# Two triangular products of a grouped convolution in five sets of matmuls instead of six

## What is computed

```python
def conv_layer(x, c, weight, c_weight, bias):          # layers 0 and 2
    out = lax.conv_general_dilated(x, weight, window_strides=(1,), padding=[(4, 4)],
              dimension_numbers=('NCH', 'OIH', 'NCH'), feature_group_count=4)
    return out + jnp.einsum('nd,od->no', c, c_weight)[:, :, None] + bias[None, :, None]

def mix_layer(x, embedding, W0, b0, W1, b1, W2, b2, weight, bias_k):   # layers 1 and 3
    h = gelu(gelu(embedding @ W0 + b0) @ W1 + b1)
    att = jax.nn.softmax(h @ W2 + b2, axis=-1)
    agg_w = jnp.einsum('bk,koi->boi', att, weight[..., 0])
    return jnp.einsum('boi,bih->boh', agg_w, x) + (att @ bias_k)[:, :, None]

x = x + conv_layer(x, ...)
x = x + mix_layer(x, ...)
x = x + conv_layer(x, ...)
x = x + mix_layer(x, ...)
```

## Time and profile before

| | |
|---|---|
| median of 3 runs | 2541.18 us (2540.11 to 2541.45) |
| the profiled execution | 2542.88 us |
| its span, first to last instruction | 2541.0 us |
| mean granted TensorE clock over the span | 0.991 of 2.4 GHz |
| PE busy | 2491.0 us (98%), 45292 matmul instructions |
| DVE busy | 2134.1 us (84%) |
| ACT busy | 1519.8 us (60%) |
| DMA engines, mean busy share | 45% |

### The profile page before, as it was taken

How to read it: one execution, slowest core, us unless ns; L and a number is a source line. 1 busy time by engine, 2 the same in 40 slices (tenths; PEclk the granted TensorE clock), 3 DMA queues, 4 the chain that set the end, 5 groups by cost and what they waited for, 6 DMA issues and landing times.

```text
span 2541.0 us, 99176 instructions
## 1 busy us (share of the span) xinstructions
PE 2491.0 (98%) x45292; PEld 1381.1 (54%) x45292; DVE 2134.1 (84%) x811; ACT 1519.8 (60%) x1113; POOL 33.6 (1%) x31
## 2 busy tenths in 40 slices
PE   5999999999999999999999999999999999999998
PEld 3444444444444455555555566666666666666665
DVE  3679888888988988988988988988888898898883
ACT  3356666666666666666666666666666666666654
POOL 5000000000000000000000000000000000000000
PEclk9899999999999999999999999999999999999999
DMA  7534445444344344444443444444444544434433
GB/s 218 199 126 157 132 126 162 125 136 153 124 147 142 124 157 131 132 154 126 140 149 124 148 140 124 155 134 125 160 128 131 158 124 142 147 124 152 136 93 117
DMA packets 185506, 357.27 MB, mean 141 GB/s; under 512 B 12714, under 2 KB 143794, under 8 KB 152634
## 3 DMA queue, kind: packets, MB, share of 16 engines
q1 hardware_dynamic: 184576, 352.37, 44.3%
q10 hardware_dynamic: 898, 4.39, 0.8%
HBM read 205.72 MB, written 150.99 MB: 140 GB/s over the span
## 4 chain that ended last, share of the span: by engine, by line
PE 96%; DVE 1%; DMA 1%; ACT 1%; issue 1%; ACTq 0%; DVEq 0%
PE psum L338 60%; PE psum L404 35%; DMA mix_dram<-y 1%; PE psum L319 1%; DVE diff L644 0%; ACT y L541 0%; PE psum L311 0%; DVE y L707 0%; ACT y L569 0%; DVE att_t L669 0%; DVE y L698 0%; ACT x L608 0%; ACT outb L590 0%; ACT shared L551 0%; ACT shared L558 0%
## 5 line engine op out<-in xcount | busy, mean ns | idle before, releaser
L338 PE MATMUL psum<-diff,prod_w 32*64 32x512 f32 x28672 | 1691.2, 590 | 9.2 <-ACT shared L558 3.8
L338 PEld LDWEIGHTS psum<-diff,prod_w 32*64 32x64 f32 x28672 | 886.9, 132 | 719.5 <-issue 436.2
L644 DVE TENSOR_TENSOR diff<-xin 128x2052 f32<-128x2052 f32 x256 | 993.4, 3934 | 297.9 <-PE psum L338 297.4
L404 PE MATMUL psum<-y,mixw 32*64 32x512 f32 x16384 | 1022.9, 591 | 6.0 <-DVE y L707 5.3
L404 PEld LDWEIGHTS psum<-y,mixw 32*64 32x64 f32 x16384 | 533.8, 132 | 386.1 <-issue 232.1
L644 DVE TENSOR_TENSOR diff<-x 128x2055 f32<-128x2055 f32 x256 | 572.3, 2315 | 9.2 <-ACT x L608 9.2
L608 ACT ACTIVATE x<-psum,bias_now 128x2048 f32<-128x2048 f32 x128 | 253.2, 1978 | 207.8 <-PE psum L404 207.8
L590 ACT ACTIVATE outb<-psum,bias_now 128x2048 f32<-128x2048 f32 x128 | 252.1, 1969 | 200.4 <-PE psum L404 191.3
L558 ACT COPY shared<-psum 128x2048 f32<-128x2048 f32 x128 | 239.1, 1868 | 189.7 <-PE psum L338 178.1
L705 DVE TENSOR_TENSOR y<-y,shared 128x2048 f32<-128x2048 f32 x128 | 295.3, 2307 | 39.6 <-ACT y L567 39.6
L707 DVE TENSOR_TENSOR y<-y,shared 128x2048 f32<-128x2048 f32 x128 | 295.4, 2307 | 1.0 <-ACT y L569 1.0
(11 more groups left out here) (63 smaller groups left out, 112.6 us busy)
## 6 DMA issues: line engine op xcount, KB each, us to landing
xin<-x SPq DMA_DIRECT2D x128, 1024.0 KB, 7.0
out<-outb SPq DMA_DIRECT2D x128, 1024.0 KB, 4.7
mixw<-mix_dram SPq DMA_DIRECT2D x512, 128.0 KB, 5.3
mix_dram<-y SPq DMA_DIRECT2D x14, 1024.0 KB, 4.8
mix_dram<-shared SPq DMA_DIRECT2D x2, 1024.0 KB, 5.1
y<-experts ACTq DMA_DIRECT2D x2, 512.0 KB, 14.6
x<-conv_w ACTq DMA_DIRECT2D x1, 768.0 KB, 19.3
shared<-conv_w ACTq DMA_DIRECT2D x1, 768.0 KB, 22.8
```

The lines of the kernel that those rows point to most:

```text
L338: return pe.matmul(psum[cols, half, g, :], prod_w[v][at, kind, s, cols], moving, start=start, stop=stop, skip_group_check=True)
L404: mm = pe.matmul(psum[cols, half, r, :], mixw[m][at, b, g, cols], y[m][at, :, g, b, :], start=g == 0, stop=g == GROUPS - 1)
L644: nc.vector.tensor_tensor(into(kind), in0, in1, op).then_inc(diff_ready[v], 1)
```

## The change

`divided_set` is replaced by `joint_set(v, s, groups)`: `ONLY_EVEN` with phase s on the output phases 0 to s, and beside it `ONLY_ODD` with phase s + 1 on the output phases s + 1 to 3. Together they are exactly 128 columns for s = 0, 1 and 2. With `ONLY_EVEN` s = 3 and `ONLY_ODD` s = 0 these are five sets. For s = 1 both parts are 64 columns wide. For s = 0 and 2 one part is 32 columns and the other 96, which is written as one tile of 64 and one of 32. A group of these two sets so has three matmuls, one of 64 and two of 32 columns. The number of matmuls of a convolution stays 112: 96 of 64 columns and 16 of 32.

```diff
-            def divided_set(v, s, groups):
-
+            def joint_set(v, s, groups):
+
+                phase = [slice(CG * r, CG * (r + 1)) for r in range(PH)]
+                even_cols = {0: (phase[0],), 1: (LOWER,), 2: (LOWER, phase[2])}[s]
+                odd_cols = {0: (phase[1], UPPER), 1: (UPPER,), 2: (phase[3],)}[s]
                 for g in groups:
-                    mm = conv_tile(v, ONLY_EVEN, A, s, g, LOWER, stop=s == 1)
-                    other = conv_tile(v, ONLY_ODD, B_HALF, s + 2, g, UPPER)
+                    for cols in even_cols:
+                        mm = conv_tile(v, ONLY_EVEN, A, s, g, cols, stop=s == 0)
+                    for cols in odd_cols:
+                        mm = conv_tile(v, ONLY_ODD, B_HALF, s + 1, g, cols)
                 return mm
...
                 wide_set(v, ONLY_EVEN, A, 3, LEADING)
                 wide_set(v, SIGNED, B_HALF, 3, TRAILING).then_inc(conv_done[v], 1)
-                wide_set(v, ONLY_EVEN, A, 2, LEADING)
+                pe.wait_ge(shared_ready[v], COPIES * n + 2)
+                joint_set(v, 2, LEADING)
                 wide_set(v, ONLY_EVEN, A, 3, TRAILING)
-                pe.wait_ge(shared_ready[v], COPIES * n + 2)
-                divided_set(v, 0, LEADING)
-                wide_set(v, ONLY_EVEN, A, 2, TRAILING)
-                divided_set(v, 1, LEADING).then_inc(conv_done[v], 1)
+                joint_set(v, 1, LEADING)
                 pe.wait_ge(shared_ready[v], COPIES * n + 3)
-                divided_set(v, 0, TRAILING)
-                wide_set(v, ONLY_ODD, B_HALF, 0, LEADING)
-                divided_set(v, 1, TRAILING).then_inc(conv_done[v], 1)
-                wide_set(v, ONLY_ODD, B_HALF, 1, LEADING, stop=True).then_inc(conv_done[v], 1)
-                wide_set(v, ONLY_ODD, B_HALF, 0, TRAILING)
+                joint_set(v, 2, TRAILING)
+                joint_set(v, 0, LEADING).then_inc(conv_done[v], 1)
+                joint_set(v, 1, TRAILING)
+                wide_set(v, ONLY_ODD, B_HALF, 0, LEADING, stop=True)
+                joint_set(v, 0, TRAILING).then_inc(conv_done[v], 1)
 
             def conv_tail(v):
-                wide_set(v, ONLY_ODD, B_HALF, 1, TRAILING, stop=True).then_inc(conv_done[v], 1)
+                wide_set(v, ONLY_ODD, B_HALF, 0, TRAILING, stop=True).then_inc(conv_done[v], 2)
```

## The result

The changed kernel takes 5782.64 us (median of 4 runs, 5774.66 to 5785.81) against 2541.31 us before: a ratio of 2.2751, with a 95% interval of 2.2712 to 2.279. The forecast was 5690 us. The profiled execution has a span of 5781.6 us and a mean granted clock of 0.695.

The account below looks back on a forecast made before the run. PE's full array was taken as the bound; 25.4 + 17.2 + 0.9 = 43.5 us a half-step instead of 18.9, 24.6 more x 128 = 3149, on 2543 gave 5692, stated as 5690 us; range 2546 to 6290.

Parts of the forecast that it names:

- What bounds the kernel: PE's steady part: all eight tiles full, no pause worth removing, 0.107 us a matmul, 18.9 us a half-step.
- Changes of width empty the array: At each of 14 places per half-step between 64 and 32 columns, all tiles drain, with a 0.09 us gap.
- The price of a run: One or two matmuls alone between width changes: 1.0 us at full clock, 1.9 at the lower level.
- The clock: Granted clock falls some 3 us into the stretch of lone runs and stays low for some 5 us behind it.
- Dense work behind the stretch: 64-column matmuls after the lone runs: 4.8 us at the lower clock level, losing 2.4 us.
- The 13 runs: Between first and last width change, 38 matmuls in 13 runs of one width: 25.4 us per half-step.
- The rest of the half-step: The other 138 matmuls of 64 columns: 14.8 us plus 2.4 for the low clock, 17.2; with the ends 0.9 more.
- the closer waits: Waits for copies L561 and L565: 0.46 to 0.55 and 0.44 to 0.53 us, claimed hidden under the forecast.
- the ends: At the first and last width change, half the array idles for one or two instructions: 0.9 us together.
- Rival 1: Convolution widths work side by side, two closer waits take the gain: 2546 to 2569 us, middle 2559; chance 0.15.
- Rival 2: Same two waits, widths side by side: waits cost less than the array gains, 2431 or 2495 us; chance 0.05.
- Rival 3: At width changes only overlapping tiles wait, 0.8 us a half-step more: 2667 us; chance 0.04.

Follow-up runs that it names:

- e9: Kernel before, with only PE's second wait for the copies of half B moved ahead of ONLY_EVEN s = 2 leading: 2603.19 us, ratio 1.0248.
- e10: Kernel before, with only the signal for half A's sums, groups 0 and 1, sent one leading half-set later: 2611.93 us, ratio 1.0283.
- e3: Kernel before, with one 64-column matmul of each convolution written as two of 32 columns: 2680.42 us, ratio 1.0546.
- e4: Kernel before, with two 64-column matmuls of each convolution each written as two of 32 columns: 2827.28 us, ratio 1.1123.
- e2: Changed kernel, with all steady-part matmuls in 32-column tiles, twice as many, and PE's loop written out: 3154.9 us, ratio 1.2412.
- e6: Kernel before, with 24 matmuls of 64 columns written as 48 of 32 in one piece, two width changes per half-step: 2657.18 us, ratio 1.0456.

## Why the prediction was right, point by point

- **What bounds the kernel.** Right. The array was full, and the single pauses of e9 and e10 showed at about their full length.
- **Changes of width empty the array, also between 32 and 64 columns.** Right, and the step that carried it all. The three places between 64 and 128 columns with their 0.09 us told it. e3 shows the same for 64 and 32: no load for 0.81 us ahead of the run and for 0.84 behind it, then 16 at once. The rule of the Trainium skill (TensorEngine Tiling (Array Packing), Key Properties), that a change of mode drains TensorE, held between 32x64 and 32x32; the timelines of the changed kernel and of e3 agree with it.
- **The price of a run.** 1.0 us at the full clock and 1.9 at the lower were forecast, 0.97 to 1.0 and 1.84 to 1.9 measured. e3 and e4 give 1.08 and 1.11 us for a run with its two changes.
- **The clock.** Right that it falls in the stretch and stays low behind it. That it fell 3.0 us after the first change in the half-step shown (3018.0 against 3015.04), as expected, is luck: no row gave the 3 us (the earlier trace rows have the fall 1.2 to 2.2 us after 93.07). In twelve half-steps of the trace the fall came 2.3 to 3.5 us after the first change, here one of the earliest and one of the latest:

```profile
536.74:563.70 26.96, 26.96 (x104) 4.72 (x108) 1.80 (x1) 2.12 (x3) 0.00 (x0) 0.50 0.00 0
2045.31:2072.20 26.89, 26.89 (x119) 5.36 (x111) 3.74 (x1) 3.89 (x3) 0.00 (x0) 0.50 0.00 0
```

  Their first changes are at 534.24 and 2041.81. Where the fall came earlier, the return to 1.00 did, too (29.6 to 31.0 us after the first change), so these half-steps have the same length within 0.2 us and the forecast lost nothing by it. Dense work behind the stretch was expected to run 4.8 us at the lower level and did so for 5.2 in the half-step shown (3040.12 to about 3045.35). What it loses there was put at 2.4 us, half of 4.8; by the counts in the earlier trace rows, 52 against 82 in 4.40, it would be 2.0. The 13 runs: 25.4 us forecast, 25.1 measured.
- **The rest of the half-step.** Forecast 17.2 + 0.9 = 18.1 us, measured 44.3 - 25.1 = 19.2. This is the term that was too small, and the step that failed in it is the sentence that the closer waits are hidden under the forecast. One is: its copy (L568) has long been made when PE gets to the mixing. The other named one stands ahead of the stretch, where nothing has slowed PE down yet. Its loads waited 0.96 us for ACT (the row at 3014.04), and e9 measures the pause alone at 0.49 us, 63 us of the whole. The prediction didn't name the third wait, for the copy of line 570; its loads waited 1.05 us (the row at 3043.18), while part of the array still worked. And the last 64-column matmul ahead of the first change (3014.04 to 3015.04) is already a run of its own, which I had counted among the dense ones. These two share the remaining 0.6 us with the 0.9 estimated for the ends; no run separates them.
- **The split of the loss.** Per half-step 25.4 us: 14.8 - 4.1 = 10.7 for the runs at the full clock, 25.1 - 14.8 = 10.3 for the lower level in them and 5.2 / 2 = 2.6 for it behind them, and 1.8 for the waits and the ends. By this sum, whose 14.8 is an estimate from runs of 1.0 us, half of the loss is the clock. The sum without it was 4026.
- **Rival 1** had the right price for the two waits that it names (0.90 to 1.08 forecast, 0.49 + 0.56 = 1.05 measured one by one), but widths don't mix freely, and it left out the third. **Rival 2** falls with e9 and e10: both waits cost over 0.41 us. **Rival 3** falls with e3.

## What to carry to other kernels

Count the places in program order where the width of TensorE's tile changes, not the tiles: here each one stopped all tiles, and a matmul that stood alone between two such places took 1.0 us for 0.107. Work of another width belongs into one block, and it has to save more than such a pair costs, here 0.9 to 1.1 us, the time of eight to ten matmuls. When a step takes work out of a full engine, look at which copies and waits were covered by just that work, and follow every signal that moves: here two of three such waits, measured one by one, cost more than the estimated gain. And PE's busy share, 98% before and 99% after, didn't show how many of its tiles work; loads that are no longer drawn ahead, and the granted clock, did.

## What was not expected of the hardware

- Narrow tiles are taken in more slowly than the array could work on them: 33 loads per us in a stretch without waits for copies (e2), where 37 would fill 16 tiles of 32 columns. With 64-column tiles 18.7 per us (9326 in 500 us) fill it, so nothing of this shows there.
- Two changes of width cost 0.91 us even around a full array (e6), far more than twice the 0.09 us of the earlier trace rows; 0.76 of it lies between the two changes.
- Tiles of one width don't keep to the order of the program among each other. Where the mixing begins, its first half-set (L404) is issued ahead of the last four matmuls of the convolution (L338), on other row groups. In the kernel before, the convolution's first instructions start at 1014.34, between the first instructions of that half-set (1014.31 and 1014.39) and ahead of its second ones, which start 0.43 us after its first:

```profile
1014.31 0.60 PE L404 MATMUL psum<-y,mixw 32*64 32x512 f32 x2
1014.34 0.61 PE L338 MATMUL psum<-diff,prod_w 32*64 32x512 f32 x4
1014.39 0.94 PE L404 MATMUL psum<-y,mixw 32*64 32x512 f32 x4
```

  At a change of width nothing of the kind was seen: all tiles waited.
